# A decoder layer on one core: 71 tiles of expert slots in place of 72, a wait for stores and four loads moved into the attention

## The chip, the core and the metric

The kernel runs on one core of a Trainium2 chip. Its time is device time in microseconds from one launch to its end. A core has five engines that run side by side and meet through semaphores: PE (TensorE, matmuls), DVE (VectorE), ACT (ScalarE), POOL (GpSimd) and SP (SyncE, which here only issues DMA transfers). ACT and POOL issue DMA transfers too.

## What is computed

One layer of a decoder, for x of 4 x 1024 tokens of width 256, all in float32:

```
x = x + self_attention(layernorm(x), Wq, bq, Wk, bk, Wv, bv, Wo, bo)   # 16 heads of 16, 4 KV heads
x = x + cross_attention(layernorm(x), ctx, mask, Wq, Wk, Wv, Wo)       # ctx: 4 x 77 tokens, 16 heads of 64
xn = layernorm(x) * ln_scale + ln_bias
probs = softmax(xn @ gate_w.T)             # 8 experts
w = top 2 of probs, each over their sum    # 0 for the other six
out = swiglu(x, sWg, sWu, sWd)             # the shared expert
for e in range(8):
    out = out + w[:, e] * swiglu(x, Wg[e], Wu[e], Wd[e])
x = x + out
```

## The kernel before

`decoder_layer` runs six stages one behind the other: `phase_qkv`, `phase_attention`, `phase_self_out`, `phase_context`, `phase_cross` and `phase_ffn`. Each is a block with one program for each engine. At a block's end stands a barrier: no engine begins the next stage before all five have ended the one before. Nothing is reordered; every engine does its instructions in the order in which they are written, and waits where a semaphore is named.

**Projections** (`phase_qkv`). Eight quads of 512 tokens go through layer norm, transposes and projections. ACT writes the high part of a projection to the buffer `part` (two halves, for even and odd quads) and DVE the low part (L229). SP then stores each to DRAM, as `q_parts` and `k_parts` (L172): three stores a quad, with the semaphores `stored` for even and odd quads. After quads 3 and 5 SP issues the loads of the attention's groups 0 and 1 (`load_group`, L86 to L90). At the end SP waits until every store has landed (L179).

**Attention** (`phase_attention`). There are 16 groups, each of one KV head and one batch. Keys and queries of a group lie in one of four slots of `KS` and `QS`. Pass A (PE L555, into `psA`) multiplies queries by keys to learn each row's maximum, which DVE takes (L504) and negates (L514). POOL splits the maxima in two parts, DVE transposes them (L492), SP stores them as `m_parts` (L435) and loads them as two more rows of `QS` (L439). Pass B (PE L565, into `psB`) then yields scores less their maximum, and ACT takes the exponential into `PT` (L536). PE multiplies by the values (L584), and ACT copies the sums to `OU` (L526), one half of a group's queries at a time. A group has 32 units of pass B, and pass A of the next group runs beside them. Only for group 0 does PE do 52 matmuls of pass A ahead of all else. SP goes through the groups in order: for each, the row copies of both halves, then `load_group` for the group after the next.

**Output projection** (`phase_self_out`). 32 tiles of 128 tokens. SP loads `Wo` (L670), `bo` (L671) and the tiles of `OU` as `OT`, in two buffers (L677). The loads of tiles 0 and 1 wait for nothing, each later one until the tile two before it has been turned. PE turns a tile (`psR`, L721), DVE divides by the sums (L737, L739), PE turns back (`psU`, L713), ACT copies (L757), PE multiplies by `Wo` (`psY`, L705), DVE adds to `X` (L746). POOL adds the bias to all of `X` (L691). After every second copy ACT issues a load of the next stage's weights (L786, L792).

**Experts** (`phase_ffn`). 24 tiles of tokens go through the shared expert while the routing is worked out; then come NTM tiles of slots, in which the tokens are sorted by expert, each expert's count filled up to a whole number of tiles; then the last 8 tiles of the shared expert. NTM is 72, the most that can be needed (71) made even, because the loop over tiles takes two at a time:

```
NTM = (TOP * B * S + NE * (P - 1)) // P
NTM += NTM % 2
```

A step of PE turns tile i (`m_psT`, L1708), multiplies tile i - 1 by two weight matrices (`m_psG`, `m_psU`, L1696), and turns and multiplies tile i - 2 (`m_psH`, L1683; `m_psY`, L1726). Around it POOL gathers each tile's rows (L1638) and adds its results to `acc` (L1646), and ACT and DVE split the third weight matrix of the tile's expert (L1941, L1892).

Of the kernel before, what the change touches and what calls it, by code (L numbers as in the profile page):

```python
# [5 lines left out]
F32 = mybir.dt.float32  # L6
# [27 lines left out]

NTM = (TOP * B * S + NE * (P - 1)) // P
NTM += NTM % 2
NSLOT = NTM * P
# [55 lines left out]

NLOAD = 16 * 2 * 5


def phase_qkv(nc, T):
# [4 lines left out]
    with ExitStack() as ctx:  # L102
# [22 lines left out]

        NQ = NT // QUAD
        XLOADS = 4
# [15 lines left out]
        va_done = sem("va_done")  # L143
        stored = [sem("stored_even"), sem("stored_odd")]
        KROWS, VROWS = slice(0, NKV * HD), slice(NKV * HD, 2 * NKV * HD)
        MS = [(2, NKV * HD), (0, P), (1, P)]
        NM = len(MS)
        NSTORE = 16 * NM
        GROUP_AT = (3, 5)
# [3 lines left out]
        def _(sp):  # L153
# [8 lines left out]
            for i in range(NQ):  # L162
# [10 lines left out]
                if i in GROUP_AT:  # L173
                    if i == GROUP_AT[0]:
                        sp.wait_ge(consts, 5)
                    load_group(sp, T, GROUP_AT.index(i), GROUP_AT.index(i) % SLOTS)

            for e in range(2):
                sp.wait_ge(stored[e], NSTORE * NQ // 2)  # L179

# [180 lines left out]
def phase_attention(nc, T):  # L361
# [6 lines left out]
    with ExitStack() as ctx:  # L368
# [5 lines left out]

        VG = sb("VG", [P, 2, TB, VW])
        PT = sb("PT", [P, 4, GH, HALF])
        half_max = sb("half_max", [P, NC, 2])
        neg_max = sb("neg_max", [P, NC])
        max_parts = sb("max_parts", [P, 2, NC], F32R)
        max_parts_t = sb("max_parts_t", [P, 2 * NC])  # L380
        zero = sb("zero_row", [P, 1, D])
        psA = ctx.enter_context(nc.psum_tensor("psA", [P, RING, HALF], F32))
        psB = ctx.enter_context(nc.psum_tensor("psB", [P, 2, 2, HALF], F32))
# [41 lines left out]
        def _(sp):  # L425
# [6 lines left out]
            def rows(i, slot, half):  # L432
# [5 lines left out]
                for r in range(2):  # L438
                    sp.dma_start(QS.bitcast(F32)[r * ROWS + KQ:r * ROWS + KM, slot, :, half * HALF:(half + 1) * HALF],  # L439
                                 m_parts[i, half, :].rearrange("(j a r n) -> r j a n", j=2, r=2, n=HALF)[r]).then_inc(rows_set[half], 16)  # L440

            for i in range(NG):
                for half in range(2):
                    rows(i, i % SLOTS, half)
                if i + 2 < NG:
                    load(i + 2, (i + 2) % SLOTS)
            for half in range(2):
                sp.wait_ge(rows_set[half], NROWS * NG)
# [73 lines left out]
        def _(act):  # L522
# [6 lines left out]
            def exps(i):  # L529
                for u in range(NU):  # L530
# [9 lines left out]
                    if u == NC + LAG - 2:  # L540
                        take_out(i, 0)

            for i in range(NG):
                exps(i)
# [89 lines left out]


def phase_self_out(nc, T):

    X, OU, ident = T["X"], T["OU"], T["ident"]
    with ExitStack() as ctx:
# [5 lines left out]

        wo = sb("wo_sb", [P, KD, D])
        bo = sb("bo_sb", [P, D])
        OT = sb("OT", [P, 2, NKV, P])
        recip = sb("recip", [P, 2, NH])
        ON = sb("ON", [P, 2, D])  # L650
        ONT = sb("ONT", [P, 2, KD, P])
        assert nc.sbuf_base <= T["context_from"]
        psR = ctx.enter_context(nc.psum_tensor("psR", [P, 2, HALF], F32))
        psU = ctx.enter_context(nc.psum_tensor("psU", [P, 2, HALF], F32))
        psY = ctx.enter_context(nc.psum_tensor("psY", [P, 2, HALF], F32))
        w_in = sem("so_w_in")
        bias_added = sem("so_bias_added")
        sums_in = [sem("so_sums_in_even"), sem("so_sums_in_odd")]
        rows_done = sem("so_rows_done")
# [8 lines left out]
        @block.sync  # L668
        def _(sp):
            sp.dma_start(wo[:, :, :], T["Wo"].rearrange("(k p) n -> p k n", p=P)).then_inc(w_in, 16)  # L670
            sp.dma_start(bo[:, :], T["bo"].rearrange("(a n) -> a n", a=1).to_broadcast([P, D])).then_inc(w_in, 16)  # L671

            def load(i, e):
                if not peeled(i, 2):

                    sp.wait_ge(rows_done, at(i, 1, -1))
                sp.dma_start(OT[:, e, :, :], OU[:, :, bass.ds(i * P, P)]).then_inc(sums_in[e], 16)  # L677

            load(0, 0)
            load(1, 1)  # L680
            with sp.Fori(1, NT // 2) as j:
                load(j * 2, 0)
                load(j * 2 + 1, 1)
            for e in range(2):
                sp.wait_ge(sums_in[e], 16 * (NT // 2))
# [728 lines left out]
def phase_ffn(nc, T):  # L1414
# [14 lines left out]
    with ExitStack() as ctx:  # L1429
# [104 lines left out]
        def steps(step, eng, beside=lambda s: None):  # L1534
# [3 lines left out]
            with eng.Fori(EARLY_TILES // 2 + 2, END // 2) as j:  # L1538
                for e in range(2):
                    step(lambda lag, j=j, e=e: (j * 2 + (e - lag), (e - lag) % 2))  # L1540
            for s in range(END, NALL + 2):
                step(lambda lag, s=s: (s - lag, (s - lag) % 2) if s - lag < NALL else None)
# [207 lines left out]
        def _(dve):  # L1750
# [106 lines left out]
            def step(tile):  # L1857
# [16 lines left out]
                if t := tile(2):  # L1874
                    i, e = t
                    dve.wait_ge(y_done, at(i, 1, 1))
                    if shared(i):
                        n = number(i)
                        bank = 0 if i < EARLY_TILES else e
                        dve.wait_ge(acc_in[e], 16 * (n // 2 + 1))  # L1880
                        dve.tensor_tensor(yt[:, n % 3, :], psY[:, bank, 0:D], yt[:, n % 3, :], ALU.add).then_inc(y_in, 1)  # L1881
# [75 lines left out]
def decoder_layer(nc, T):  # L1957
    with ExitStack() as ctx:
# [22 lines left out]
        with ExitStack() as attention:  # L1981
            sb(attention, "VA", [P, NG, TB, VW])
            sb(attention, "OU", [P, NKV, B * S])
            with ExitStack() as stacks:

                sb(stacks, "QS", [P, SLOTS, GH // 2, S], F32R)
                sb(stacks, "KS", [P, SLOTS, S], F32R)
                T["loaded"] = [stacks.enter_context(nc.semaphore(f"loaded_{e}")) for e in ("even", "odd")]
                phase_qkv(nc, T)
                phase_attention(nc, T)  # L1990
            context_places(nc, T)
            T["cx_in"] = ctx.enter_context(nc.semaphore("cx_in"))
            phase_self_out(nc, T)
# [63 lines left out]
```

## Time and profile before

| | us |
|---|---|
| median of three runs | 1801.6 |
| lowest and highest | 1800.39 and 1805.86 |
| the profiled execution, its own time | 1806.33 |
| its span, from the first to the last instruction | 1804.6 |
| PE busy in it | 1708.7 (95%) |
| DVE busy | 1390.4 (77%) |
| ACT busy | 1116.0 (62%) |
| POOL busy | 363.6 (20%) |

Times in the profile are microseconds from the start of the span. "A <- B" behind a number is what ended an engine's idle time. PEclk is the granted clock of PE as a share of 2.4 GHz; 0.50 is 1.2 GHz. A matmul's duration is modelled, so a busy PE isn't always one at its peak.

### The profile page before, as it was taken

How to read it: one execution, taken by the hardware profiler on the slowest of the kernel's cores; microseconds unless marked ns; L12 is line 12 of the kernel's file. 1: busy time of each engine (PE TensorE's matmuls, PEld its weight loads, DVE VectorE, ACT ScalarE, POOL GpSimd, SP SyncE). 2: the span in 40 equal slices, each digit the busy share in tenths (PEclk: the TensorE clock that was granted, in tenths of full speed). 3: DMA queues.
4: the chain of work that ended last, by engine and by line, in shares of the span. 5: the costliest groups of instructions: out<-in, count | busy, mean ns of one | idle time of the engine just before them, and what ended most of it. 6: DMA issues, size and time to landing. Idle time of an engine off the chain costs nothing. (4 is left out here: it accounts for less than half of the span.)

```text
span 1804.6 us, 36497 instructions
## 1 busy us (share of the span) xinstructions
PE 1708.7 (95%) x11980; PEld 1115.3 (62%) x11981; DVE 1390.4 (77%) x2656; ACT 1116.0 (62%) x2308; POOL 363.6 (20%) x433
## 2 busy tenths in 40 slices
PE   6699999999999999978879999997899999999998
PEld 3343333333333333346578999996798888888887
DVE  5498999999999999524578999984658666666664
ACT  4327888888888888821467888884226555555552
POOL 2100000000000000040023222221130455555540
PEclk9958999999999999999999999998999999999999
DMA  5701112111111111054210211114515233333335
GB/s 189 204 2 29 30 31 44 38 30 30 29 29 29 29 30 29 3 162 134 113 41 29 89 46 71 33 33 135 181 59 170 47 52 52 53 52 52 52 56 161
DMA packets 96015, 120.69 MB, mean 67 GB/s; under 512 B 19019, under 2 KB 76799, under 8 KB 94783
## 3 DMA queue, kind: packets, MB, share of 16 engines
q1 hardware_dynamic: 77936, 95.15, 19.1%
q0 software_dynamic: 13920, 19.15, 6.7%
q10 hardware_dynamic: 4047, 4.91, 0.9%
q8 instruction: 70, 1.15, 0.3%
q14 instruction: 42, 0.34, 0.1%
HBM read 71.38 MB, written 42.53 MB: 63 GB/s over the span
## 5 line engine op out<-in xcount | busy, mean ns | idle before, releaser
L504 DVE TENSOR_REDUCE half_max<-psA 128x1 f32<-128x512 f32 x1024 | 633.7, 683 | 25.2 <-PE psA L555 24.2
L536 ACT ACTIVATE PT<-psB 128x1024 f32<-128x1024 f32 x512 | 518.6, 1026 | 137.3 <-PE psB L565 137.3
L555 PE MATMUL psA<-KS,QS 48*128 48x512 f32 x1024 | 402.2, 473 | 11.4 <-PEq L102 9.6
L565 PE MATMUL psB<-QS,KS 50*128 50x512 f32 x1024 | 369.9, 459 | 0.2 <-ACT PT L536 0.2
L584 PE MATMUL psO<-PT,VG 128*32 128x256 f32 x4096 | 331.1, 396 | 4.5 <-ACT OU L526 0.4
L555 PEld LDWEIGHTS psA<-KS,QS 48*128 48x128 f32 x1024 | 165.1, 193 | 232.8 <-DVE half_max L504 167.7
L584 PEld LDWEIGHTS psO<-PT,VG 128*32 128x32 f32 x4096 | 82.3, 108 | 194.5 <-issue 118.3
L1726 PE MATMUL m_psY<-swd_high,m_hT 128*128 128x256 f32 x832 | 174.9, 293 | 11.0 <-DVE m_hT L1861 9.3
L1331 ACT ACTIVATE x_probs<-x_scores,x_neg_max 128x77 f32<-128x77 f32 x512 | 176.3, 358 | 3.4 <-DVE x_neg_max L1237 3.2
L565 PEld LDWEIGHTS psB<-QS,KS 50*128 50x128 f32 x1024 | 147.2, 188 | 13.1 <-ACT PT L536 10.6
L1726 PEld LDWEIGHTS m_psY<-swd_high,m_hT 128*128 128x128 f32 x832 | 135.7, 190 | 21.8 <-DVE m_hT L1861 12.5
L1181 PE MATMUL psYx<-VO,x_ET 128*128 (+1 forms) x640 | 146.0, 383 | 1.4 <-ACT x_ET L1354 0.9
L1646 POOL DMA_INDIRECT acc<-m_y,tokens x72 | 114.3, 1588 | 160.3 <-DVE m_y L1888 160.3
L473 POOL CAST max_parts<-neg_max 128x16 fp32r<-128x16 f32 x32 | 6.3, 198 | 632.9 <-DVE neg_max L514 632.9
L1941 ACT ACTIVATE swd_high<-WD 128x1024 fp32r x72 | 76.3, 1060 | 91.0 <-PE m_psY L1726 91.0
L1181 PEld LDWEIGHTS psYx<-VO,x_ET 128*128 128x128 f32 x640 | 119.1, 190 | 17.4 <-issue 2.3
L1132 PE MATMUL psS<-cx_mx,x_xnT 128*128 (+2 forms) x576 | 124.6, 363 | 3.9 <-DVE x_xnT L1284 3.9
L1892 DVE TENSOR_TENSOR swd_low<-WD,swd_high 128x1024 fp32r<-128x1024 f32 x72 | 88.2, 1226 | 44.5 <-ACT swd_high L1941 44.5
L1726 PE MATMUL m_psY<-swd_low,m_hT 128*128 128x256 f32 x416 | 117.3, 282 | 0.0
L1696 PE MATMUL m_psG<-m_X_split,m_xT 128*128 x288 | 108.1, 416 | 0.0
L1132 PEld LDWEIGHTS psS<-cx_mx,x_xnT 128*128 128x128 f32 x576 | 99.1, 191 | 12.4 <-DVE x_xnT L1284 4.6
L1932 ACT ACTIVATE m_xT<-m_psT 128x256 fp32r<-128x256 f32 x104 | 40.1, 385 | 106.2 <-PE m_psT L1708 106.2
(213 smaller groups left out, 2759.6 us busy)
## 6 DMA issues: line engine op xcount, KB each, us to landing
QS<-q_parts SPq DMA_DIRECT2D x96, 128.0 KB
q_parts<-part SPq DMA_DIRECT2D x16, 512.0 KB, 3.8
OT<-OU SPq DMA_DIRECT2D x32, 256.0 KB, 2.6
mx_kept<-cx_mx SPq DMA_DIRECT2D x4, 1232.0 KB, 10.1
cx_mx<-mx_kept SPq DMA_DIRECT2D x4, 1232.0 KB, 7.0
KS<-k_parts SPq DMA_DIRECT2D x32, 128.0 KB
xf_rows<-XF SPq DMA_DIRECT2D x32, 128.0 KB, 1.7
acc<-X SPq DMA_DIRECT2D x32, 128.0 KB, 1.8
```

Of the source, the lines that this page charges most:

```text
L504: dve.tensor_reduce(half_max[:, h * (TB // 2) + t % (TB // 2), n:n + 1], psA[:, bank_of(slot, 2 * v + r), :], axis=AX.X, op=ALU.max).then_ ...
L536: act.activation(PT[:, k % 4, 2 * a:2 * a + 2, :].rearrange("p h n -> p (h n)"), psB[:, u % 2, :, :].rearrange("p a n -> p (a n)"), ACT.Ex ...
L555: pe.matmul(psA[:, bank_of(slot, m), :], QS[top:top + KQ, slot, h // 2, t * P:(t + 1) * P], KS[top:top + KQ, slot, n * HALF:(n + 1) * HALF ...
L565: mm = pe.matmul(psB[:, u % 2, r, :], KS[top:top + KM, slot, c * P:(c + 1) * P], QS[top:top + KM, slot, a, half * HALF:(half + 1) * HALF], ...
L584: mm = pe.matmul(psO[h * VW:(h + 1) * VW, 0, cols], VG[:, e, c, :], PT[:, k % 4, h, cols], start=(c == 0 and q == 0), stop=(c == TB - 1 an ...
L1132: mm = pe.matmul(psS[:, n, 0:heads * SC], xnT[a][:, e, k, :], MX[:, i // TB % 2, b, k, first * SC:(first + heads) * SC], start=(k == 0 and ...
L1181: mm = pe.matmul(psY[:, 0, 0:D], ET[:, c, :], VO[:, i // TB, c, :], start=(c == 0), stop=(c == NPK - 1))
L1331: act.activation(PX[:, e, cols], SX[:, e, cols], ACT.Exp, scale=XSCALE, bias=neg_max[:, e, h:h + 1], accum_out=row_sum[:, e, h:h + 1]).the ...
L1646: pool.indirect_dma_start(out=acc, out_offset=bass.IndirectOffsetOnAxis(ap=tokens[:, of_slots(i):of_slots(i) + 1], axis=0), in_=yt[:, i % ...
L1696: mm = pe.matmul(bank[:, e, :], xT[a][:, e, k, :], w, start=(k == 0 and (a, b) == PRODUCTS[0]), stop=(k == KD - 1 and (a, b) == PRODUCTS[-1]))
L1726: mm = pe.matmul(psY[:, e_bank, 0:D], HL[a][:, e, k, :], SHARED[2][b][:, k, :], start=(k == 0 and (a, b) == PRODUCTS[0]), stop=(k == KF - ...
L1892: dve.tensor_tensor(SHARED[2][1][:, :, :], WD[:, x, :, :], SHARED[2][0][:, :, :], ALU.subtract).then_inc(wd_low, 1)
```

## The change

- NTM is 71. The loop over pairs of tiles ends one pair earlier, and the odd last step stands behind it, written out. The tiles of the shared expert behind the slots have changed parity, so DVE picks their semaphore by the tile's own number.
- SP no longer waits for the stores at the end of the projections. The wait stands in the attention, on SP ahead of the first row copies and on ACT ahead of the first exponential, because `PT` lies where `part` was. The two large buffers of the attention, `VG` and `PT`, are placed behind the small ones, so that those don't lie on `part`.
- SP issues the loads of `Wo`, `bo` and the first two tiles of `OT` at the end of its attention program, as soon as groups 0 to 13 have been multiplied by their values and the sums of groups 0 to 12 are in `OU`. The three buffers lie in slots of `QS` that are free by then.

```diff
-NTM = (TOP * B * S + NE * (P - 1)) // P
-NTM += NTM % 2
+NTM = TOP * B * S // P + NE - 1
...
-        stored = [sem("stored_even"), sem("stored_odd")]
+        stored = T["q_stored"]
...
-            for e in range(2):
-                sp.wait_ge(stored[e], NSTORE * NQ // 2)
...
-        VG = sb("VG", [P, 2, TB, VW])
-        PT = sb("PT", [P, 4, GH, HALF])
...
         zero = sb("zero_row", [P, 1, D])
+        VG = sb("VG", [P, 2, TB, VW])
+        PT = sb("PT", [P, 4, GH, HALF])
...
+            for e in range(2):
+                sp.wait_ge(T["q_stored"][e], NSTORE * NQ // 2)
             for i in range(NG):
                 for half in range(2):
                     rows(i, i % SLOTS, half)
                 if i + 2 < NG:
                     load(i + 2, (i + 2) % SLOTS)
+            sp.wait_ge(pv_done, NC * (NG - 2))
+            sp.wait_ge(out_copied, 2 * (NG - B + 1))
+            load_self_out(sp, T)
...
+            for e in range(2):
+                act.wait_ge(T["q_stored"][e], NSTORE * NQ // 2)
             for i in range(NG):
                 exps(i)
...
+def load_rows(eng, T, i, e):
+    eng.dma_start(T["OT"][:, e, :, :], T["OU"][:, :, bass.ds(i * P, P)]).then_inc(T["so_sums_in"][e], 16)
+
+
+def load_self_out(eng, T):
+    eng.dma_start(T["wo_sb"][:, :, :], T["Wo"].rearrange("(k p) n -> p k n", p=P)).then_inc(T["so_w_in"], 16)
+    eng.dma_start(T["bo_sb"][:, :], T["bo"].rearrange("(a n) -> a n", a=1).to_broadcast([P, D])).then_inc(T["so_w_in"], 16)
+    for e in range(2):
+        load_rows(eng, T, e, e)
...
-            sp.dma_start(wo[:, :, :], T["Wo"].rearrange("(k p) n -> p k n", p=P)).then_inc(w_in, 16)
-            sp.dma_start(bo[:, :], T["bo"].rearrange("(a n) -> a n", a=1).to_broadcast([P, D])).then_inc(w_in, 16)
-
             def load(i, e):
-                if not peeled(i, 2):
-
-                    sp.wait_ge(rows_done, at(i, 1, -1))
-                sp.dma_start(OT[:, e, :, :], OU[:, :, bass.ds(i * P, P)]).then_inc(sums_in[e], 16)
-
-            load(0, 0)
-            load(1, 1)
+                sp.wait_ge(rows_done, at(i, 1, -1))
+                load_rows(sp, T, i, e)
+
             with sp.Fori(1, NT // 2) as j:
...
-            for s in range(END, NALL + 2):
+            for s in range(END // 2 * 2, NALL + 2):
...
-                        dve.wait_ge(acc_in[e], 16 * (n // 2 + 1))
+                        dve.wait_ge(acc_in[n % 2], 16 * (n // 2 + 1))
```

Where the rows of SP's program stand. First, SP from the last quad's stores into the attention, before the change; a branch marks the end of a stage's program and the start of the next:

```order
L172 DMA k_parts<-part 64x2x512 [waits low_done]
L172 DMA q_parts<-part 128x2x512 [waits low_done] x2
L102 UNCONDITIONAL_BRANCH [waits stored_odd,stored_even]
L424 UNCONDITIONAL_BRANCH [waits barrier_Pool_Activation_PE_DVE_SP_release]
L435 DMA m_parts<-max_parts_t 4x32x32 [waits mt_done]
```

And with the change, where `q_stored` is the new name of `stored`:

```order
L172 DMA k_parts<-part 64x2x512 [waits low_done]
L172 DMA q_parts<-part 128x2x512 [waits low_done] x2
L104 UNCONDITIONAL_BRANCH
L421 UNCONDITIONAL_BRANCH [waits barrier_Pool_Activation_PE_DVE_SP_release]
L432 DMA m_parts<-max_parts_t 4x32x32 [waits mt_done,q_stored_odd,q_stored_even]
```

The wait for the stores has moved from ahead of the barrier to the first store of the maxima, which waits for DVE's transposition (`mt_done`) as well.

Second, SP from the last rows of the attention into the output projection, before:

```order
L439 DMA QS<-m_parts 2x2x512
L368 UNCONDITIONAL_BRANCH [waits rows_set_second,rows_set_first]
L668 UNCONDITIONAL_BRANCH [waits barrier_Pool_Activation_PE_DVE_SP_release]
L670 DMA wo_sb<-in_Wo 128x2x256
L671 DMA bo_sb<-in_bo 128x256
L677 DMA OT<-OU 128x4x128 x2
L681 UNCONDITIONAL_BRANCH
```

And with the change:

```order
L436 DMA QS<-m_parts 2x2x512
L655 DMA wo_sb<-in_Wo 128x2x256 [waits out_copied,pv_done]
L656 DMA bo_sb<-in_bo 128x256
L651 DMA OT<-OU 128x4x128 x2
L365 UNCONDITIONAL_BRANCH [waits rows_set_second,rows_set_first]
L690 UNCONDITIONAL_BRANCH [waits barrier_Pool_Activation_PE_DVE_SP_release]
L696 UNCONDITIONAL_BRANCH
```

Four transfers have moved from behind the barrier to ahead of it, behind the last row copies; the loop that loads the other 30 tiles follows as before.

## Rows read from the trace of the kernel before

**Rows 1.** The page: PE's share of the span, and its clock in 40 slices.

```profile
PE 1708.7 (95%) x11980; PEld 1115.3 (62%) x11981; DVE 1390.4 (77%) x2656; ACT 1116.0 (62%) x2308; POOL 363.6 (20%) x433
...
PEclk9958999999999999999999999998999999999999
```

**Rows 2.** Timeline, 76 to 88.5: start, duration, instructions merged, idle before.

```profile
77.24 2.08 SPq L172 DMA_DIRECT2D q_parts<-part  x2
77.35 0.46 PE L352 MATMUL psV<-ident,vT 64*128 64x64 f32 x4
...
78.84 0.41 DVE L247 COPY VA<-psV 128x256 f32<-128x256 f32 x1
...
87.42 1.19 PE L555 MATMUL psA<-KS,QS 48*128 48x512 f32 x3 [9.61 <-PEq L102]
```

**Rows 3.** Waits of SP, 60 to 130: total, times, longest.

```profile
SPq L179 <- DMA q_parts<-part: 7.6, 1, 7.6
```

**Rows 4.** Windows: length, busy PE, PEld, DVE, ACT, POOL, PEclk, DMA share, GB/s.

```profile
80.00:85.00 5.00, 0.00 (x0) 0.00 (x0) 0.00 (x0) 0.00 (x0) 0.00 (x0) 0.74 0.34 133
...
140.00:145.00 5.00, 5.00 (x32) 1.52 (x32) 3.26 (x6) 2.67 (x3) 0.00 (x0) 0.50 0.25 61
...
150.00:155.00 5.00, 4.86 (x49) 1.69 (x49) 5.00 (x9) 3.79 (x5) 0.00 (x0) 1.00 0.19 45
```

**Rows 5.** Timeline of DVE, 86 to 130.

```profile
88.22 19.22 DVE L504 TENSOR_REDUCE half_max<-psA 128x1 f32<-128x512 f32 x32 [8.96 <-PE psA L555]
...
113.81 12.00 DVE L504 TENSOR_REDUCE half_max<-psA 128x1 f32<-128x512 f32 x20
```

**Rows 6.** Timeline of ACT, 124 to 152.

```profile
124.94 1.02 ACT L536 ACTIVATE PT<-psB 128x1024 f32<-128x1024 f32 x1 [0.17 <-PE psB L565]
...
146.54 1.02 ACT L536 ACTIVATE PT<-psB 128x1024 f32<-128x1024 f32 x1 [1.14 <-PE psB L565]
...
149.40 1.02 ACT L536 ACTIVATE PT<-psB 128x1024 f32<-128x1024 f32 x1 [0.23 <-PE psB L565]
150.63 1.02 ACT L536 ACTIVATE PT<-psB 128x1024 f32<-128x1024 f32 x1 [0.20 <-PE psB L565]
```

**Rows 7.** Timeline, 773 to 783.

```profile
774.60 0.60 ACT L526 ACTIVATE OU<-psO 128x512 f32<-128x512 f32 x1 [1.30 <-PE psO L584]
775.47 0.41 SPq L670 DMA_DIRECT2D wo_sb<-in_Wo  x1
...
780.04 1.09 PE L721 MATMUL psR<-ident,OT 128*128 128x128 f32 x4 [5.51 <-DMA OT<-OU]
```

**Rows 8.** Chain that ended last, 1430 to 1470: start, duration, piece; seven such rows.

```profile
1435.11 1.65 PE m_psY L1726 x12
...
1465.19 1.66 PE m_psY L1726 x12
```

**Rows 9.** Windows, columns as in rows 4.

```profile
755.00:760.00 5.00, 5.00 (x54) 1.72 (x50) 0.00 (x0) 4.66 (x5) 0.00 (x0) 1.00 0.01 3
...
850.00:855.00 5.00, 3.35 (x16) 2.28 (x17) 0.42 (x1) 0.73 (x2) 0.00 (x0) 0.88 0.01 2
```

**Rows 10.** Timelines of ACT and of SP, 740 to 800.

```profile
743.35 0.60 ACT L526 ACTIVATE OU<-psO 128x512 f32<-128x512 f32 x1 [0.78 <-PE psO L584]
...
749.73 1.23 SPq L439 DMA_DIRECT2D QS<-m_parts  x2
```

**Rows 11.** DMA issues (KB each, us to landing) and waits, 774 to 860.

```profile
OT<-OU SPq DMA_DIRECT2D x32, 256.0 KB, 2.6
...
wo_sb<-in_Wo SPq DMA_DIRECT2D x1, 256.0 KB, 2.8
...
PE psR L721 <- DMA OT<-OU: 12.5, 6, 5.5
```

**Rows 12.** Timeline of PE, 774 to 800.

```profile
783.27 1.92 PE L705 MATMUL psY<-wo_sb,ONT 128*128 128x256 f32 x4
...
785.41 0.66 PE L721 MATMUL psR<-ident,OT 128*128 128x128 f32 x4
786.09 1.13 PE L705 MATMUL psY<-wo_sb,ONT 128*128 128x256 f32 x4
```

More of the change, by code:

```diff
@@ L94 @@
 NLOAD = 16 * 2 * 5
+NQ = NT // QUAD
+NM = 3
+NSTORE = 16 * NM
 def phase_qkv(nc, T):
@@ L124, in phase_qkv @@
         psV = ctx.enter_context(nc.psum_tensor("psV", [P, 2, HALF], F32))
-        NQ = NT // QUAD
         XLOADS = 4
@@ L143, in phase_qkv @@
         va_done = sem("va_done")
-        stored = [sem("stored_even"), sem("stored_odd")]
+        stored = T["q_stored"]
         KROWS, VROWS = slice(0, NKV * HD), slice(NKV * HD, 2 * NKV * HD)
         MS = [(2, NKV * HD), (0, P), (1, P)]
-        NM = len(MS)
-        NSTORE = 16 * NM
+        assert NM == len(MS)
         GROUP_AT = (3, 5)
@@ L633, with self_out_places @@
 NEG_RAW = NEG / XSCALE
+def self_out_places(nc, T):
+    offset = T["place"]["QS"] + 4608
+    for name, shape in (("wo_sb", [P, KD, D]), ("bo_sb", [P, D]), ("OT", [P, 2, NKV, P])):
+        T[name] = nc.alloc_sbuf_tensor_at(name, shape, F32, offset=offset)
+        offset += 4 * math.prod(shape[1:])
+    assert offset <= T["place"]["QS"] + 4 * 2 * (GH // 2) * S
+def load_rows(eng, T, i, e):
[5 more added lines that the diff above has]
+        load_rows(eng, T, e, e)
 def phase_self_out(nc, T):
-    X, OU, ident = T["X"], T["OU"], T["ident"]
+    X, ident = T["X"], T["ident"]
     with ExitStack() as ctx:
@@ L644, in sem @@
             return ctx.enter_context(nc.semaphore(name))
-        wo = sb("wo_sb", [P, KD, D])
-        bo = sb("bo_sb", [P, D])
-        OT = sb("OT", [P, 2, NKV, P])
+        wo, bo, OT, w_in, sums_in = (T[k] for k in ("wo_sb", "bo_sb", "OT", "so_w_in", "so_sums_in"))
         recip = sb("recip", [P, 2, NH])
@@ L651, in phase_self_out @@
         ONT = sb("ONT", [P, 2, KD, P])
+        assert nc.sbuf_base <= T["place"]["QS"] + 4608
         assert nc.sbuf_base <= T["context_from"]
@@ L655, in phase_self_out @@
         psY = ctx.enter_context(nc.psum_tensor("psY", [P, 2, HALF], F32))
-        w_in = sem("so_w_in")
         bias_added = sem("so_bias_added")
-        sums_in = [sem("so_sums_in_even"), sem("so_sums_in_odd")]
         rows_done = sem("so_rows_done")
@@ L1983, in decoder_layer @@
             sb(attention, "OU", [P, NKV, B * S])
+            T["so_w_in"] = attention.enter_context(nc.semaphore("so_w_in"))
+            T["so_sums_in"] = [attention.enter_context(nc.semaphore(f"so_sums_in_{e}")) for e in ("even", "odd")]
             with ExitStack() as stacks:
@@ L1987, in decoder_layer @@
                 sb(stacks, "KS", [P, SLOTS, S], F32R)
+                T["q_stored"] = [stacks.enter_context(nc.semaphore(f"q_stored_{e}")) for e in ("even", "odd")]
                 T["loaded"] = [stacks.enter_context(nc.semaphore(f"loaded_{e}")) for e in ("even", "odd")]
+                self_out_places(nc, T)
                 phase_qkv(nc, T)
```

## Prediction

> **What bounds the kernel now.** I read the page first, then the timeline at the two borders the change touches, then the waits, then the granted clock there. The page says that PE is busy 95% of the span and that its clock is at 2.4 GHz except in three of the forty slices [rows 1]. So a gain can come from three places: work taken off PE, borders between stages where PE stands still, and stretches at 1.2 GHz.
>
> The first border is the end of the projections. PE's last instruction there starts at 77.35, DVE's last copy ends at 78.84 + 0.41 = 79.25, and SP issues its last stores until 77.24 + 2.08 = 79.32. PE's first instruction of the attention starts at 87.42, after 9.61 us idle [rows 2]. In between only one wait ends: SP waited 7.6 us for the stores `q_parts<-part` to land [rows 3]. No engine may pass the border before SP.
>
> Behind it the clock matters. It falls to 1.2 GHz between 80 and 85, while PE stands still, and is still there at 140 to 145, though PE is busy 5.00 of 5 us; at 150 to 155 it is back at 2.4 [rows 4]. The first 52 score matmuls (pass A) lose nothing by that, because DVE is the bound there: 32 reductions in 19.22 us and 20 in 12.00 us are 0.60 us each, back to back [rows 5]. The exponentials that follow lose: at 1.2 GHz ACT starts one every 2.16 us (124.94 to 146.54 holds ten such steps), at 2.4 GHz every 1.23 us (149.40 to 150.63) [rows 6]. The slow clock costs 0.93 us a unit, 9.3 us in all in this execution.
>
> The second border is the end of the attention. ACT's last copy ends at 774.60 + 0.60 = 775.20, SP issues the load of `wo_sb` at 775.47, and PE starts at 780.04, after waiting for OT [rows 7].
>
> The third place is the expert stage: from 1435.11 to 1465.19 PE does six tiles of slots, 5.01 us each, with no gap [rows 8].
>
> **The change part by part.**
>
> *One tile of slots less.* Every tile is computed whatever is in it, so 71 in place of 72 saves PE one period, 5.0 us [rows 8]. With it go one gather, one accumulating store and one copy of each weight part, all beside PE. The last slot tile now stands behind the loop instead of in it, with the same instructions; the one-hot matmuls are 142 columns wide in place of 144, which I cost at nothing. Bounds 4.9 to 5.2.
>
> *The wait for the stores moved.* SP now waits for them ahead of the attention's first `m_parts` store, which also needs all of half 0's maxima; ACT waits for them ahead of its first exponential. In this execution the landing came 7.6 us after 79.3, at 86.9. SP's first need of the row is after 32 + 10 reductions of 0.60 us, some 25 us after the attention's start, and ACT's is later still, so both waits are over before they count. If the stores came 18 us later still, they would count. Nothing else on SP is queued behind that wait but these rows. POOL's two zero-row stores go out earlier, beside the end of the stores, and nobody waits for them. So the border opens when SP is through with issuing at 79.32, plus what a border takes: the second one took 775.47 - 775.20 = 0.27 us [rows 7], and SP's own step a little more. PE starts at about 79.8 in place of 87.42: **7.6 us**. Bounds 7.0 and 8.1 (the whole 87.42 - 79.32).
>
> *Does PE's clock now hold over this border?* The idle time shrinks from 9.6 to about 2 us. No row shows pass A alone at 2.4 GHz. For "it holds": the clock fell only after 80, with PE idle since 77.8 [rows 2, 4]. Against: through all of pass A, with 31 us of it in the trace, PE did not get the clock back, nor in 20 us of full units behind it [rows 4, 6]. Also, in 850 to 855 the mean is 0.88: the clock dipped although PE was at work for 3.35 of those 5 us [rows 9]. So work alone is no surety, and in pass A PE stops for DVE after each matmul. I take the nearer rows and forecast the same slow stretch, moved ahead by 7.6 us. Bounds: 9.3 us more gain if it holds, and as much loss if the clock stays low for ten units longer.
>
> The Trainium skill (TensorE: Matmul & The Clock Gate, "The HAM clock gate") says of this that "the default state is throttled, and activity releases the throttle". Taken at its word, a PE that is busy without a break would not be left at 1.2 GHz, and a border of 2 us would keep it at 2.4; the time would then be that of the first rival. The row at 140 to 145 speaks against that reading.
>
> *The first loads of the output projection moved.* SP issues `wo_sb`, `bo_sb` and two OT tiles (256 + 128 + 2 x 256 KB) behind its last row copies, which start at 749.73. The counts it waits for are then met: ACT's copy at 743.35 is of group 14, and it needs group 12 [rows 10]. The DMA engines are at 0.01 of their time in 755 to 760 [rows 9], and such a load lands in 2.6 to 2.8 us [rows 11], so all is in by about 757, 18 us before the end of the attention. PE starts at about 775.5 in place of 780.04: 4.5 us. POOL's bias sums begin earlier too and stay beside. Then the ramp: the third tile's psR came at 785.41, and on the way there PE ran at 1.2 GHz, with 1.92 us for a psY that takes 1.13 at 2.4 [rows 12] and 1.09 for a psR that takes 0.66 [rows 7, 12]. If the clock holds over a border of 1 us, 0.43 + 0.79 and a little more in the psU are won, about 1.5 us. It may not hold (the dip at 850 again [rows 9]), so I take half, 0.8. Together **5.3 us**; bounds 4.5 and 6.0.
>
> What is late next is the loop's own OT loads: each is issued only when the tile two before it has been read, so they move with PE, and ACT's context loads are issued after ACT's copies, so they move too. Nothing is added to the queues behind 775: four DMAs are taken away.
>
> **Sum.** 7.6 + 5.3 + 5.0 = 17.9 us. The profiled execution took 1806.33 us (span 1804.6), so it would come to 1788.4. It is 4.7 us above the median of the runs shown, 1801.6, and above each of them. The result will be a median, so I take the sum off that: 1783.7, **1784 us**.
>
> **Rivals.**
> 1. *The clock holds through pass A.* Place: from 79.8 on. For and against are above. The units that ran at 2.16 us run at 1.23: 1806.3 - 17.9 - 9.3 = 1779.1.
> 2. *The output projection gives its gain back.* PE waited 12.5 us for OT in six places, of which 5.5 at the border [rows 11]; if those transfers set the stage's end and don't move with PE, 5.3 us are lost again: 1789.0 from the median. Against: every one of them is issued behind work that moves.
> 3. *The border of the projections doesn't open.* The wait moves, but something else holds an engine, such as the first group's keys and queries, which PE waits for before pass A and whose landing no view lists. Then 7.6 us are missing: 1791.3. Against: in the trace PE goes on at once when SP does.
> 4. *The clock comes back later than before.* This is the one that could end slower than before. Place: the units of groups 0 and 1. Price 0.93 us a unit. It decides from 19 more slow units on (17.9 / 0.93). With all 32 units of group 1 slow as well it is 29.8 us: 1783.7 + 29.8 = 1813.5. For it: no row shows what brings the clock back. Against: in this trace it took ten units, and the three runs lie within 5.5 us, so such long stretches can't be common.
>
> That 71 tiles might be too few is no rival: 8192 rows in eight groups, each filled up to 128, need at most 64 + 7.
>
> **How the numbers follow.** Forecast 0.74; rival 1 0.08; rival 2 0.09; rival 3 0.04; rival 4 0.05. The forecast's own range, by the bounds of its terms and a clock that is back up to five units earlier or later, is 1779 to 1788.5. With rivals 1 and 2 it is 1778 to 1790, which leaves out rivals 3 and 4. A difference of 0.3%, 5.4 us, is about what a measurement of this kernel can tell from none. The forecast and rivals 1 to 3 are all faster by more: 0.95. Rival 4 splits into 0.03 for within 0.3% and 0.02 for slower.
>
> **What would show it.** Right: PE's first psA about 2 us after the projections' last PE work; no wait of SP there; the clock at 1.2 GHz for pass A and some units; the first psR 0.3 us after ACT's last copy, without a wait for OT; the loads of `wo_sb` and OT near 751; six tiles in 30.1 us as before, and one fewer; each stage behind a border shifted as a whole. Wrong: an idle gap of more than 4 us at either border; a psR wait for OT that is new or longer in the loop; exponentials more than 2 us apart for more than 20 units or for none; an expert stage that is not 5 us shorter.

## The result and the profile after

The changed kernel took 1786.26 us in the median of its first four runs (1781.99 to 1790.44), the kernel before 1802.65 beside it (four runs): ratio 0.9908, 95% interval 0.9879 to 0.9936. Twice more, six runs each, it took 1782.91 and 1782.39 us, ratios 0.9882 (0.9856 to 0.9909) and 0.9874 (0.9840 to 0.9907). So it is 1% faster; 1784 was forecast. The profiled execution is the fastest of the first four, 1781.99 us with a span of 1780.3, where that of before (1806.33) was slower than all four timed runs beside it. The difference of these two profiles is 24.3 us, and a part of it is chance, as will be seen.

The page of the kernel after, PE's line and its clock in 40 slices; these answer to [rows 1]:

```profile
PE 1694.7 (95%) x11950; PEld 1108.4 (62%) x11951; DVE 1386.3 (78%) x2651; ACT 1112.4 (62%) x2304; POOL 360.2 (20%) x431
...
PEclk9969999999999999999999999998999999999999
```

PE's busy time falls by 14.0 us, of which 5.0 are the tile. The other 9.0 lie in the attention, where PE does the same work but is busy for 671.7 us in place of 680.6, because less of it runs at 1.2 GHz: the third and fourth slice show 6 and 9 tenths in place of 5 and 8.

The timeline of after at the first border, 74 to 90 us, against [rows 2]:

```profile
77.28 2.08 SPq L172 DMA_DIRECT2D q_parts<-part  x2
77.39 0.46 PE L349 MATMUL psV<-ident,vT 64*128 64x64 f32 x4
...
78.88 0.41 DVE L244 COPY VA<-psV 128x256 f32<-128x256 f32 x1
...
79.80 0.70 PE L559 MATMUL psA<-KS,QS 48*128 48x512 f32 x3 [1.96 <-PEq L104]
```

PE stands still for 1.96 us, not 9.61, and begins the attention 7.62 us earlier. SP's last stores are issued until 79.36, and the stage opens 0.44 us later. Among SP's waits from 60 to 130 us there is none for the stores any more; that of 7.6 us [rows 3] is gone and not moved.

The granted clock and the exponentials behind pass A, windows (columns as in [rows 4]) and ACT's timeline:

```profile
80.00:85.00 5.00, 4.23 (x10) 1.75 (x8) 4.70 (x8) 0.00 (x0) 1.88 (x4) 0.75 0.56 208
...
115.00:120.00 5.00, 5.00 (x28) 1.93 (x26) 4.15 (x7) 3.54 (x4) 0.00 (x0) 0.50 0.00 0
120.00:125.00 5.00, 5.00 (x52) 1.83 (x48) 4.54 (x10) 3.71 (x5) 0.81 (x3) 0.99 0.01 3
```

```profile
117.06 1.02 ACT L538 ACTIVATE PT<-psB 128x1024 f32<-128x1024 f32 x1 [0.20 <-PE psB L569]
119.22 1.02 ACT L538 ACTIVATE PT<-psB 128x1024 f32<-128x1024 f32 x1 [1.14 <-PE psB L569]
120.88 1.02 ACT L538 ACTIVATE PT<-psB 128x1024 f32<-128x1024 f32 x1 [0.64 <-PE psB L569]
122.12 1.02 ACT L538 ACTIVATE PT<-psB 128x1024 f32<-128x1024 f32 x1 [0.21 <-PE psB L569]
```

The clock falls where it fell before, between 80 and 85 us, though PE now works there. It is back at 120, and one step of 2.16 us stands here in place of ten [rows 6].

The second border, 756 to 768 us, and SP's loads ahead of it, against [rows 7, 10, 12]:

```profile
758.39 0.60 ACT L528 ACTIVATE OU<-psO 128x512 f32<-128x512 f32 x1 [1.30 <-PE psO L588]
...
759.45 0.63 PE L736 MATMUL psR<-ident,OT 128*128 128x128 f32 x4 [1.12 <-PEq L365]
...
761.79 2.07 PE L720 MATMUL psY<-wo_sb,ONT 128*128 128x256 f32 x4
```

```profile
733.54 1.23 SPq L436 DMA_DIRECT2D QS<-m_parts  x2
734.89 0.41 SPq L655 DMA_DIRECT2D wo_sb<-in_Wo  x1
735.35 0.47 SPq L656 DMA_DIRECT2D bo_sb<-in_bo  x1
735.86 1.41 SPq L651 DMA_DIRECT2D OT<-OU  x2
```

The loads are issued 23 us ahead of the border, right behind the last row copies. PE waits 1.12 us there and for no DMA. The psY at 761.79 is slow, 2.07 us in place of 1.13: the clock dips here as well.

At the end of the expert stage something is longer than before. The chain that ended last, of before and of after:

```profile
1762.68 4.65 DMA swd_low<-swd_kept
...
1767.37 1.69 PE m_psY L1726 x12
```

```profile
1736.66 6.32 DMA swd_low<-swd_kept
...
1743.03 1.69 PE m_psY L1741 x12
```

This is the reload of the shared expert's third weight matrix behind the last tile of slots. PE waits for it 1.7 us in before and 3.4 in after.

The two profiles part by part, from the starts and ends of PE's work in the traces:

| stretch | before | after | gain |
|---|---|---|---|
| start to the attention's first psA | 87.42 | 79.80 | 7.62 |
| first psA to the end of the last psO | 687.11 | 678.52 | 8.59 |
| from there to the next stage's first work (psPc) | 77.48 | 72.65 | 4.83 |
| from there to the 25th m_psT | 542.79 | 542.89 | -0.10 |
| 25th to 91st m_psT | 330.56 | 330.58 | -0.02 |
| 91st to the last m_psT | 66.33 | 62.90 | 3.43 |
| the rest | 12.92 | 12.93 | -0.01 |

Three rows are those that the change was to move: 7.6, 4.8 and 3.4. The second, the largest, is one in which it removes nothing.

### The profile page after: what moved, and what is told of

It is laid out like the page before. It is cut to its first block and busy times, and to the rows that moved or that the text cites. A ratio compares the mean times of both kernels' runs of the same rounds, so it can differ in the third digit from the quotient of the medians.

```text
span 1780.3 us, 36372 instructions
## 1 busy us (share of the span) xinstructions
PE 1694.7 (95%) x11950; PEld 1108.4 (62%) x11951; DVE 1386.3 (78%) x2651; ACT 1112.4 (62%) x2304; POOL 360.2 (20%) x431
## 5 line engine op out<-in xcount | busy, mean ns | idle before, releaser
L559 PE MATMUL psA<-KS,QS 48*128 48x512 f32 x1024 | 397.1, 466 | 4.1 <-PEq L104 2.0
L569 PE MATMUL psB<-QS,KS 50*128 50x512 f32 x1024 | 365.3, 454 | 0.2 <-ACT PT L538 0.2
L588 PE MATMUL psO<-PT,VG 128*32 128x256 f32 x4096 | 327.2, 392 | 4.5 <-ACT OU L528 0.4
```

The source lines that it names most:

```text
L559: pe.matmul(psA[:, bank_of(slot, m), :], QS[top:top + KQ, slot, h // 2, t * P:(t + 1) * P], KS[top:top + KQ, slot, n * HALF:(n + 1) * HALF ...
L569: mm = pe.matmul(psB[:, u % 2, r, :], KS[top:top + KM, slot, c * P:(c + 1) * P], QS[top:top + KM, slot, a, half * HALF:(half + 1) * HALF], ...
L588: mm = pe.matmul(psO[h * VW:(h + 1) * VW, 0, cols], VG[:, e, c, :], PT[:, k % 4, h, cols], start=(c == 0 and q == 0), stop=(c == TB - 1 an ...
```

## The experiments

The theory: the terms of the sum are right, each in its place; the attention's 8.6 us are the time at which the clock happens to come back, and the missing 1.6 us of the tile are the longer reload. The rivals: an earlier start of pass A brings the clock back earlier; the odd number of tiles makes the reload long; what the change leaves beside its three parts is worth something.

**The changed kernel again**, without an edit.

> The changed kernel once more, nothing edited. Theory (three shifts that add up, and a clock that comes back at a different moment in every execution): the first psA at 79.8, the first psR 1.1 us after PE's last work of the attention and the tail's PE stall as stages of the code stay where they were, but the clock's return after pass A lies elsewhere than at 120, anywhere between 115 and 150, and the end of the attention moves with it by 0.93 us for each unit that ran at 1.2 GHz. Time about 1786, runs 4 to 9 us apart. Rival (the earlier start itself brings the clock back early): the clock is back at 120 again, the attention's end lies within 1 us of 759.0 again.

1782.91 us (1780.34 to 1788.58). Its profiled run took 1788.58. Windows:

```profile
120.00:125.00 5.00, 5.00 (x34) 1.59 (x32) 3.33 (x6) 2.40 (x3) 0.40 (x1) 0.50 0.01 3
...
135.00:140.00 5.00, 5.00 (x37) 1.65 (x36) 3.61 (x6) 2.83 (x3) 0.00 (x0) 0.67 0.97 151
```

The same program, and the clock is back at 138.3 us in place of 120.1. The exponentials from 116.00 to 137.61 are ten steps of 2.16, as many as in the kernel before, and the attention takes 686.78 us, 0.3 less than before. So the 8.6 us do not belong to the change.

**One part at a time**: the other two parts undone in the changed code, three kernels. The edits, in the order in which they are put together:

```diff
  # undo the wait: at the end of SP's projections
+ for e in range(2):
+     sp.wait_ge(stored[e], NSTORE * NQ // 2)
  # undo the loads: out of the attention, back into SP's phase_self_out
- sp.wait_ge(pv_done, NC * (NG - 2))
- sp.wait_ge(out_copied, 2 * (NG - B + 1))
- load_self_out(sp, T)
  ...
+ load_self_out(sp, T)
  # undo the tile
- NTM = TOP * B * S // P + NE - 1
+ NTM = TOP * B * S // P + NE
```

> Only the wait for the stores is moved; 72 tiles, and the output projection's first loads behind the barrier as before. Theory: first psA 7.6 us earlier, at 79.8; from there on everything as before but for the clock's return; second border 5.5 us of idle PE as before; expert stage as before. Median 7.6 us under the kernel before. Rival (the earlier start brings the clock back early too): 16 us under it, with the first group's slow units gone.

> Only the four loads are moved; 72 tiles, and the wait for the stores at the end of the projections as before. Theory: PE starts the output projection about 1.1 us after its last work of the attention in place of 5.5, so the median is 4.4 us under the kernel before; up to 1 more if the clock doesn't dip in the ramp. Rival (the stage's transfers set its end): first psR 4.4 us earlier, but the next stage's first psPc no earlier, and no gain.

> Only the tile is dropped (71 of 72); both moves undone. Theory: one period of 5.0 us less up to the last tiles of slots; what the changed kernel's profile lost there (PE waited 3.4 us for the reload of swd_low in place of 1.7) is a matter of that execution's transfers, so the stall lies between 1.7 and 3.4 and the median 3.4 to 5.0 us under the kernel before. Rival (the odd last tile makes the reload slower): the stall is 3.4 us again, with a reload of 6.3 us, and the median is 3.4 us under.

| kernel (12 runs each) | median us | ratio | interval |
|---|---|---|---|
| wait alone | 1797.03 | 0.9956 | 0.9937 to 0.9975 |
| loads alone | 1796.48 | 0.9953 | 0.9935 to 0.9971 |
| tile alone | 1796.56 | 0.9949 | 0.9928 to 0.9971 |

Before took 1804.15 beside them. The traces show that each part does its own work and none of another's. With the wait alone PE starts pass A after 1.96 us and waits for OT at the second border; with the loads alone it is the other way round (the rows of the wait alone come first):

```profile
79.92 0.70 PE L556 MATMUL psA<-KS,QS 48*128 48x512 f32 x3 [1.96 <-PEq L104]
...
771.32 1.09 PE L735 MATMUL psR<-ident,OT 128*128 128x128 f32 x4 [5.55 <-DMA OT<-OU]
```

```profile
87.77 1.19 PE L562 MATMUL psA<-KS,QS 48*128 48x512 f32 x3 [9.75 <-PEq L104]
...
776.00 0.63 PE L739 MATMUL psR<-ident,OT 128*128 128x128 f32 x4 [1.12 <-PEq L368]
...
778.35 1.13 PE L723 MATMUL psY<-wo_sb,ONT 128*128 128x256 f32 x4
```

In this last profile the clock holds from the last psO to psPc (the first psY takes 1.13), and the stretch is 71.47 us, 6.0 less than before. The medians say less: each interval is some 7 us wide, and 7.1, 7.7 and 7.6 us add up to 22, a little more than the parts give together. The loads and the tile gained more in the median than was expected of them (4.4 to 5.4 and 3.4 to 5.0 us; both intervals begin at 5.2 us). No stretch of their traces shows this excess, so the sizes of the parts are read from the traces.

**All three undone**, by the same edits.

> The changed kernel with its three parts undone: the wait for the last stores back at the end of the projections, the output projection's loads back in its own program, 72 tiles. What is left of the change is the place of the tiles in memory, the semaphores that are counted apart, and the one-hot work that goes with the number of tiles. Theory: these are worth nothing, and the time is that of the kernel before within 2 us (ratio 0.999 to 1.001), its first score product at 87.4 us and the output projection 77 to 78 us long. Rival, since the three parts one by one gained 7.1, 7.7 and 7.6 us in the median, 22 together, where all at once gained 16 to 21: what is left is itself worth 2 to 4 us, and the time is 0.9975 to 0.999 of before.

1804.04 us (1799.62 to 1815.62, 12 runs) against 1803.53; ratio 1.0009 (0.9989 to 1.0028). What is left beside the three parts is worth nothing that can be measured (the interval leaves room for a gain of 2 us at most), and that rival falls. This kernel starts pass A at 87.69 us, as late as before, but its clock was back at 130.3 and its attention took 679.60 us. So the early return is not tied to the early start either.

**73 tiles**: `NTM = TOP * B * S // P + NE + 1`.

> The changed kernel with 73 tiles. In the three profiles with 71 tiles the reload of the shared down weights at the end of the expert stage took 6.32, 6.47 and 6.45 us from its issue to landing, in the three with 72 it took 4.65, 4.73 and 4.55. Theory: the loop of two steps ends one step ahead of the last tile where their number is odd, so that the code behind it is fetched while the reload runs; then 73 tiles show a reload of 6.3 to 6.5 us, and the time is the changed kernel's plus two tiles at 5.0, 1793 to 1797. Rival: the number or the place of the tiles in time sets it; then 73 tiles give 4.5 to 4.8 us, and 1791 to 1795.

1797.30 us (1791.45 to 1806.32, 10 runs), ratio 0.9968 (0.9944 to 0.9991). The reload took 4.69 us with an odd number of tiles, so an odd number doesn't make it long in every execution. From the 91st to the last m_psT it took 71.39 us, two tiles at 5.0 more than the 61.3 of 71 tiles with a short reload. The median lies above both ranges that were named, by 0.3 us and by 2.3; that the scatter of the clock did this is likely but not shown.

**The loop ends at the last tile**, with one more step written out ahead of it.

```diff
- for s in range(EARLY_TILES + 4):
+ odd = END % 2
+ for s in range(EARLY_TILES + 4 + odd):
...
-         step(lambda lag, j=j, e=e: (j * 2 + (e - lag), (e - lag) % 2))
- for s in range(END // 2 * 2, NALL + 2):
+         step(lambda lag, j=j, e=e: (j * 2 + (odd + e - lag), (odd + e - lag) % 2))
+ for s in range(END, NALL + 2):
```

> The changed kernel with one more step of the expert stage written out ahead of the loop, so that the loop of two steps ends with the last of the 71 tiles, as it does with 72. Theory: the reload of the shared down weights falls from 6.3 to 4.6 us, TensorE's wait there from 3.4 to 1.7, and with it the loss of the clock behind the wait (3.4 us at 1.2 GHz, 1.7 us lost, in two of the three profiles with 71 tiles); the median is 1.7 to 3.4 us under the changed kernel's. Rival: the reload is long for another reason; it stays at 6.3 to 6.5 us and the time at the changed kernel's within 1 us.

1785.51 us (1779.90 to 1789.97), ratio 0.9902 (0.9874 to 0.9930). The reload took 4.76 us and PE's wait 1.8, as the theory had it, and the last stretch took 61.34 us, 5.0 less than before. But 73 tiles had the same short reload without this edit. So both kernels were run again:

> The changed kernel once more, unaltered, beside the version whose loop ends at the last tile. Two things are open: whether the reload of the shared down weights is long in every execution of this program (6.32 and 6.47 us in its two profiles; 4.6 to 4.8 in the seven profiles of the kernels with other code around it, 6.45 with the tile alone), and whether the time between the two versions can be measured. Theory: the place of a code fetch beside the reload belongs to the program, so the reload takes 6.3 to 6.5 us again, with a fetch of 16384 bytes still under way when its second half is issued. Rival: it is chance, and 4.6 to 4.8 us appear here too. The time is 1782 to 1787 under both.

> The version whose loop ends at the last of 71 tiles, once more. Theory: reload 4.6 to 4.8 us, TensorE's wait there 1.7 to 1.9; its median lies 1.7 to 3.4 us under that of the changed kernel on the same chip. Rival: the scatter that the clock brings into each execution, some 9 us, covers it, and the two medians cannot be told apart.

The changed kernel took 1782.39 us (1780.18 to 1785.24, six runs), the other 1787.55 (1780.66 to 1798.87, ten runs; ratio 0.9904, 0.9873 to 0.9935). The reload in the two profiles, from the chain of each, first of the changed kernel and then of the other:

```profile
1741.56 4.68 DMA swd_low<-swd_kept
```

```profile
1741.90 7.14 DMA swd_low<-swd_kept
```

The theories have changed places: the program that had shown 6.32 and 6.47 shows 4.68, and the one written to keep the reload short shows 7.14. One program shows it both long and short, so it differs by chance between executions, and this edit doesn't keep it short. What makes it long stays open. In the four long ones SP's issue of the second half took 0.88 to 1.50 us in place of 0.43 to 0.53, but in the changed kernel's third profile it took 0.86 and the reload was short.

**More work for PE in pass A.** Since the largest part of the scatter is the clock behind pass A, three kernels add products that nobody reads. The first adds plain f32 products of 128 columns:

```diff
  # PE, end of the projections
+ for n in range(4):
+     pe.matmul(psT[:, 0, 0:D], ident[:, :], X[:, 0, :], start=True, stop=True)
  # PE, attention: behind each of the first 52 score products and in the first four units
+ pe.matmul(psO[:, 0, 0:n], T["ident"][:, :], T["X"][:, 0, 0:n], start=True, stop=True)
```

> The changed kernel with products added on TensorE that nobody reads: four of 256 columns after the last transposition of the projections, one of 128 columns behind each of the 50 score products of pass A's first stretch, one of 256 columns in each of the first four units. Theory: the clock of pass A falls because TensorE has too little to do there, and when it comes back differs from execution to execution (120.1 us in one profile of the changed kernel, 138.3 in another, attention's end 758.99 against 766.16). Then the granted clock stays at 2.4 GHz from 74 to 140 us, every unit takes 1.24 us, psO's last product ends at 756 to 758 us, and the median is 1777 to 1780 against 1782.9 and 1786.3 of the changed kernel. Rival: the clock falls in answer to the start of pass A, whatever TensorE does; then it still stands at 1.2 GHz for 37 us or more, the added products only cost, and the median is 1783 to 1790.

1827.91 us (1825.29 to 1836.54), ratio 1.0144 (1.0113 to 1.0175): 24 us slower than the kernel before. The first stretch of pass A has 52 score products, not 50. Windows:

```profile
85.00:90.00 5.00, 5.00 (x12) 2.81 (x11) 2.57 (x5) 0.00 (x0) 0.00 (x0) 0.52 0.05 19
100.00:105.00 5.00, 5.00 (x12) 2.79 (x11) 2.55 (x4) 0.00 (x0) 0.00 (x0) 0.50 0.00 0
170.00:175.00 5.00, 5.00 (x34) 1.60 (x32) 3.26 (x6) 2.56 (x3) 0.00 (x0) 0.50 0.02 3
```

PE went from the projections into pass A with a gap of 0.30 us and was busy 5.00 of 5 us from there on. The clock fell all the same, at 85.2, and stayed at 1.2 GHz until 177.4. PE became the bound of pass A, which took 71.3 us in place of 31. The other two kernels (on top of the loop edit) add products in the score products' own type, of 128 rows in one and of 48 rows, the first tile's once more, in the other:

```diff
+ pe.matmul(psO[:, 0, :], KS[:, 0, 0:P], KS[:, 0, 0:HALF], start=True, stop=True)
  # or
+ pe.matmul(psO[:, 0, :], QS[0:KQ, 0, 0, 0:P], KS[0:KQ, 0, 0:HALF], start=True, stop=True)
```

> The kernel whose loop ends at the last tile, with other spare products than before: one behind each of the 50 score products of pass A's first stretch and one in each of the first four units, of 128 rows and 512 columns, in the type of the score products and not in plain f32. The f32 products of 128 columns, one behind each, kept TensorE listed busy from 73.5 to 177.4 us, and the clock still stood at 1.2 GHz from 85.2 to 177.4 us. Theory: it is the kind of the work that counts, and full-height products in the score products' type keep the clock at 2.4 GHz or bring it back within a few us; then pass A stays VectorE's at 31 us, no unit takes over 1.3 us, attention's last product ends 676 us or less behind the first, and the median is 1775 to 1780, against 1785.5 without the products. Rival: the clock falls in pass A whatever TensorE does; then each pair of products takes 0.85 us at 1.2 GHz in place of 0.6, pass A ends some 10 us later, and the median is 1790 to 1830.

> As the run beside it, but the spare product is the score product of the first tile once more: 48 rows, 512 columns, so that TensorE does twice as much of what pass A has it do already. Theory: if the clock answers to the time that TensorE works in products of this type, whatever their height, it stays at 2.4 GHz here as well, median 1775 to 1780. If the height counts, it falls at 80 to 85 us as before, pass A ends some 10 us later because TensorE is its bound then, and the median is 1790 or more. Rival to both: the clock falls in both runs, and nothing that is added here holds it.

With 128 rows 1833.31 us (1824.11 to 1836.77), ratio 1.0152 (1.0122 to 1.0183); with 48 rows 1787.28 (1782.78 to 1793.42), ratio 0.9914 (0.9888 to 0.9941). Windows of the first and then of the second:

```profile
84.00:89.00 5.00, 5.00 (x8) 1.94 (x8) 2.08 (x4) 0.00 (x0) 0.00 (x0) 0.50 0.10 37
...
175.00:180.00 5.00, 5.00 (x32) 1.46 (x30) 3.37 (x7) 2.72 (x3) 0.00 (x0) 0.50 0.03 6
```

```profile
84.00:89.00 5.00, 5.00 (x18) 4.12 (x17) 5.00 (x10) 0.00 (x0) 0.00 (x0) 0.50 0.06 23
```

The clock fell in both, at 83.3 and 81.5 us, and was back at 182.2 and 136.1. The rival to both theories holds: nothing that was added kept it up. What brings it back, and what decides when, stays open.

## Why the prediction was right

**The rows over the profiles.** Eleven profiles (all but those with added products), part by part as in the table above. "Low" is how long the first stretch at 1.2 GHz lasted, "projection" runs from the last psO to the first psPc, "tail" from the 91st to the last m_psT:

| profile | pass A starts after | low | attention | projection | reload | tail |
|---|---|---|---|---|---|---|
| before | 9.61 | 64.8 | 687.11 | 77.48 | 4.65 | 66.33 |
| all undone | 9.79 | 47.8 | 679.60 | 77.48 | 4.81 | 68.07 |
| loads alone | 9.75 | 64.8 | 687.11 | 71.47 | 4.55 | 66.22 |
| tile alone | 9.81 | 68.3 | 688.03 | 77.24 | 6.45 | 64.65 |
| wait alone | 1.96 | 54.6 | 685.85 | 77.89 | 4.73 | 67.93 |
| after, first | 1.96 | 37.6 | 678.52 | 72.65 | 6.32 | 62.90 |
| after, second | 1.96 | 58.0 | 686.78 | 72.76 | 6.47 | 64.61 |
| after, third | 1.96 | 58.0 | 686.79 | 70.98 | 4.68 | 61.27 |
| loop edit, first | 1.96 | 44.4 | 681.30 | 71.66 | 4.76 | 61.34 |
| loop edit, second | 1.95 | 47.8 | 683.04 | 72.99 | 7.14 | 65.25 |
| 73 tiles | 1.96 | 58.0 | 686.90 | 71.23 | 4.69 | 71.39 |

*The first border*: 7.6 us forecast; the gap is 1.95 or 1.96 us wherever the wait is moved and 9.6 to 9.8 wherever it is not, 7.65 to 7.86 less. Right to 0.3 us, with the same 2 us of gap that were worked out from SP's last issue.

*The output projection*: 5.3 forecast, bounds 4.5 and 6.0. Where the loads are moved the stretch takes 70.98 to 72.99 us, where they are not 77.24 to 77.89. Against before's 77.48 that is 4.5 to 6.5 us. The border's part is 4.4 (5.51 us of PE's wait become 1.12). The rest goes with the clock. In three of the seven profiles with the loads moved PE stays at 2.4 GHz from the last psO to psPc, and the stretch takes 70.98 to 71.47 us, 6.0 to 6.5 less than before's. In the other four it drops to 1.2 GHz once, for 3.4 us, and takes 71.66 to 72.99, 4.5 to 5.8 less. The drop need not fall on the ramp: in the second profile of after the first psY is fast and one 7 us later is slow.

```profile
768.97 1.13 PE L720 MATMUL psY<-wo_sb,ONT 128*128 128x256 f32 x4
...
776.55 1.87 PE L720 MATMUL psY<-wo_sb,ONT 128*128 128x256 f32 x4
```

That the clock may or may not hold there was the forecast's reason for taking half, and both happen; that it could also drop further on was not foreseen. The upper bound was too low, by 0.3 and 0.5 us, in two of the seven profiles.

*One tile*: 5.0 us. This term was right, and yet the first profile showed 3.4. The table tells why. With a short reload and no dip of the clock the tail takes 66.2 to 66.3 us with 72 tiles and 61.3 with 71, 5.0 apart. A long reload adds its excess (6.32 - 4.7 = 1.6 in the first profile of after). And a wait of PE there is followed in some executions by 3.4 us at 1.2 GHz, which cost 1.7 more: 68.07 with all undone, 64.61 in the second of after. The dip comes with 71 tiles and with 72. The long reload isn't fixed by the number of tiles, since kernels with 71 show both. But all four long ones are among the nine profiles with 71 tiles (the three with added products have 4.74 to 4.83 us), and none among the five with 72 or 73, so that 71 makes it more frequent isn't excluded. The prediction didn't speak of this wait at all.

*The clock*: "the same slow stretch, moved ahead by 7.6 us". Its end did that in the second and third profile of after, 138.3 us against 147.2, with the same ten slow steps. In seven of the eleven profiles the clock was back 57 to 62 us after the first psA, wherever pass A began, and in the other four after 40 to 51. The start of the slow stretch did not move: it stays at 80 to 83 us whether PE stands still there or has begun pass A. The count of slow steps also isn't a property of the kernel: one in the first profile of after, four in the loop edit's first, ten in the second and third of after. The forecast's own range allowed five steps earlier or later; the first profile of after, nine earlier, lies outside. This one step was too narrow, by some 4 us in a single execution, and a median covers it. A smaller effect of the earlier start isn't excluded: the attention takes 684.2 us on average in the seven profiles with the wait moved and 685.5 in the other four, and one program alone spreads over 8.3. The prediction's first reading, that PE is at 2.4 GHz except in three slices, was too coarse as well: a 9 stands for 90% or more, and in before PE was also at 1.2 GHz for 17 us from 1236 on.

The page "TensorE: Matmul & The Clock Gate" of the Trainium skill ("The HAM clock gate") says that activity releases the throttle. By that, the three kernels with added products should have kept or regained 2.4 GHz, and PE's rows at 0.50 with 5.00 of 5 us busy speak against it here, as the rows at 140 to 145 did [rows 4].

*The sum and what it was taken off.* 17.9 us off the median, 1801.6. The 16 runs of the changed kernel have a median of 1783.0 us (1780.18 to 1790.44). That 1784 came so close is in part luck: all 82 timed runs of before have a median of 1803.6, so the three runs lay 2.0 too low, and the gain between these medians is 20.6 us, 2.7 more than forecast. The two differences nearly cancel. What the traces show for the three terms is 7.7, 5.6 on average and 5.0, 18.3 together; the intervals of the three sets of runs all contain 17.9, so that the rest is more than scatter isn't shown. The profiled execution of before was one with a late clock; off its own 1806.33 the sum would have given 1788.4, so the choice of the median was the better one. In one set of runs of before, 1796.43 us went with a mean granted clock of 0.977 and 1815.44 with 0.963. That spread is what the parts are to be told from.

*The rivals.* The clock that holds through pass A (1): in none of the profiles. Its 1779.1 was taken off the profiled 1806.3 and not, like the forecast, off the median, which would have given 1774.4, below the range. The output projection that gives its gain back (2): PE waits for OT on the way for 6.8 us in five places in after, against 12.5 in six [rows 11], and all that is gone is the 5.5 at the border. The border that doesn't open (3): gone with the first table. The clock that comes back later (4): the longest in a profile of after, 58.0 us, holds ten slow steps, as many as before's 64.8; runs that ended slower than before were not seen. Its 29.8 us count the 32 units of group 1 but not the 18 or so of group 0 that come before them, another 17 us.

**What beats both kernels**: none of the versions tried. The loop edit (1785.51 and 1787.55), alone or with the products of 48 rows (1787.28), can't be told from the changed kernel or is a little slower; the others are slower.

## What to carry to other kernels

A wait that orders memory belongs ahead of the first instruction that reads that memory, not at the end of the stage that writes it: moved there it cost nothing, and the border gave back its whole 7.6 us; the same holds for loads that can be issued ahead of a border. Judge such terms stretch by stretch and in several profiles: a tile worth 5.0 us showed as 3.4, 1.7 or 5.1 in single pairs of profiles, and 8.3 of the 8.6 us that the attention had gained in the first pair were gone in the next execution. A stretch that agrees can do so by chance too: from psPc to the 25th m_psT, where the change moves nothing, the eleven profiles lie between 540.5 and 543.4 us, and the first pair differs by 0.10. Take a sum off a median, and don't build on work that is added to hold the clock up before a row has shown that it does.

## What the runs showed of the hardware

- A TensorE that is listed as busy without a break can stay at 1.2 GHz: 92 us of it, from 85.2 to 177.4, with plain f32 products added between the score products, and 99 with products of 128 rows. The clock fell within 6 us of pass A's start in every profile in which PE went into pass A at once.
- When it comes back differs by 18 us between executions of one program (120.1 and 138.3), 8.3 us in the attention's length.
- Products of 128 rows between those of 48 rows are dear, plain f32 ones of 128 columns (reductions 0.84 to 0.85 us apart at 2.4 GHz, 1.45 at 1.2) as well as those of 512 columns in the score products' type. DVE's reductions of the scores show the pace, first with the latter added (0.86 us apart while the clock is at 2.4 GHz, 1.38 and then 1.45 from the fall on), then with that of 48 rows, where 32 of them take 20.02 us, 0.63 each, though the clock is mostly at 1.2 GHz.:

```profile
81.55 0.69 DVE L506 TENSOR_REDUCE half_max<-psA 128x1 f32<-128x512 f32 x1 [0.16 <-PE psA L559]
82.41 0.69 DVE L506 TENSOR_REDUCE half_max<-psA 128x1 f32<-128x512 f32 x1 [0.16 <-PE psA L559]
83.27 0.69 DVE L506 TENSOR_REDUCE half_max<-psA 128x1 f32<-128x512 f32 x1 [0.17 <-PE psA L559]
84.65 0.69 DVE L506 TENSOR_REDUCE half_max<-psA 128x1 f32<-128x512 f32 x1 [0.69 <-PE psA L559]
```

```profile
79.83 20.02 DVE L506 TENSOR_REDUCE half_max<-psA 128x1 f32<-128x512 f32 x32 [1.01 <-PE psA L559]
```

- One transfer of 512 KB, issued at the same place of the same program, landed after 4.68 us in one execution and 6.47 in another.
